# First score tile of a query half made for plain and latent keys together; first half of the latent keys rotated one head ahead

## The reference

```python
q  = rope(heads(x @ w_q))                  # 32 heads
k  = rope(heads(x @ w_k)); v = x @ w_v     # 8 heads, each used by 4 query heads
lk = rope(heads((x @ w_lq) @ w_lk))        # 32 latent key heads, from a rank-128 projection
lv = heads(x @ w_lv)                       # 32 latent value heads
out = causal_attn(q, k, v) @ w_o + causal_attn(q, lk, lv) @ w_lo
x = x + out                                # then a small layer with a routed low-rank term
```

## Time and profile before

| | |
|---|---|
| median of 3 runs | 2036.75 us (2035.94 to 2037.59) |
| profiled execution | 2036.75 us, span 2035.0 us, granted PE clock 0.998 |
| PE busy | 99% of the span |
| DVE, ACT, POOL busy | 72%, 59%, 44% |
| DMA | 15.7% of 16 engines' span |

### The profile page before, as it was taken

How to read it: one execution, slowest core, us unless ns; L and a number is a source line. 1 busy time by engine, 2 the same in 40 slices (tenths; PEclk the granted TensorE clock), 3 DMA queues, 4 the chain that set the end, 5 groups by cost and what they waited for, 6 DMA issues and landing times.

```text
span 2035.0 us, 33416 instructions
## 1 busy us (share of the span) xinstructions
PE 2018.2 (99%) x11716; PEld 1753.1 (86%) x11716; DVE 1457.1 (72%) x2884; ACT 1203.7 (59%) x2505; POOL 889.9 (44%) x684
## 2 busy tenths in 40 slices
PE   8999999999999999999999999999999999999989
PEld 7888888888888888888888888888888888888877
DVE  7677776776777767777677776777776776777777
ACT  4666556565565656666566565666566565565651
POOL 5444544444443454444534454444544444443422
PEclk9999999999999999999999999999999999999999
DMA  3111111111111111112111111111111111111031
GB/s 108 47 34 44 48 28 38 34 49 37 38 39 39 33 44 37 44 28 49 33 44 37 39 39 28 49 34 44 48 28 41 32 49 39 37 39 38 23 68 42
DMA packets 101797, 83.78 MB, mean 41 GB/s; under 512 B 28152, under 2 KB 73848, under 8 KB 101632
## 3 DMA queue, kind: packets, MB, share of 16 engines
q1 hardware_dynamic: 101632, 81.65, 15.7%
HBM read 79.26 MB, written 2.36 MB: 40 GB/s over the span
## 4 chain that ended last, share of the span: by engine, by line
PE 97%; DVE 2%; ACT 1%; POOL 0%; issue 0%; DMA 0%; DVEq 0%; ACTq 0%
PE bankT L587 13%; PE scores L514 12%; PE scores L516 12%; PE scores L515 12%; PE bankX L514 9%; PE bankX L516 9%; PE bankX L515 9%; PE bankO L516 7%; PE bankO L515 7%; PE bankO L514 7%; PE scores L707 0%; PE scores L553 0%; DVE rot_half L1124 0%; DVE xnT_lo L1097 0%; ACT probs L876 0%
## 5 line engine op out<-in xcount | busy, mean ns | idle before, releaser
L815 ACT ACTIVATE PT_hi<-bankT 128x512 fp32r<-128x512 f32 (+2 forms) x640 | 337.5, 533 | 310.7 <-PE bankO L516 275.5
L1113 DVE TENSOR_TENSOR PT_lo<-bankT,PT_hi 128x512 fp32r<-128x512 f32 (+2 forms) x640 | 388.1, 607 | 175.7 <-ACT PT_hi L815 173.1
L876 ACT ACTIVATE probs<-probs,nmax 128x128 f32<-128x128 f32 (+7 forms) x512 | 393.9, 771 | 129.8 <-DVE nmax L1107 129.7
L1107 DVE CUSTOM_DVE_ANT_0 probs<-scores,mask 128x128 f32<-128x128 f32 (+7 forms) x512 | 379.2, 750 | 69.3 <-PE scores L516 68.0
L587 PE MATMUL bankT<-ident,probs 128*128 128x128 f32 x2304 | 382.7, 275 | 6.8 <-ACT probs L876 5.0
L587 PEld LDWEIGHTS bankT<-ident,probs 128*128 128x128 f32 x2304 | 279.6, 140 | 67.9 <-DVE PT_lo L1113 11.7
L1369 POOL TENSOR_TENSOR rot<-rot,cos 128x512 f32<-128x512 f32 x144 | 186.9, 1298 | 256.6 <-DVE rot_half L1124 256.6
L1363 POOL TENSOR_TENSOR OT_lo<-o_raw,OT_hi 128x512 fp32r<-128x512 f32 x63 | 98.3, 1560 | 319.9 <-ACT OT_hi L815 319.9
L815 ACT ACTIVATE OT_hi<-o_raw 128x512 fp32r<-128x512 f32 x128 | 146.7, 1146 | 139.7 <-DVE o_raw L1182 139.7
L1371 POOL TENSOR_TENSOR rot<-rot,rot_half 128x512 f32<-128x512 f32 x144 | 199.9, 1388 | 11.3
L1123 DVE TENSOR_TENSOR rot_half<-rot,sin 64x512 f32<-64x512 f32 x144 | 99.5, 691 | 135.3 <-ACT rot L815 132.3
(11 more groups left out here) (304 smaller groups left out, 5334.0 us busy)
## 6 DMA issues: line engine op xcount, KB each, us to landing
inv_b<-inverses SPq DMA_DIRECT2D x128, 256.0 KB, 3.9
stage<-in_L_attn_w_q SPq DMA_DIRECT2D x32, 256.0 KB, 4.8
stage<-in_L_attn_w_lv SPq DMA_DIRECT2D x32, 256.0 KB, 2.9
stage<-in_L_attn_w_o SPq DMA_DIRECT2D x32, 256.0 KB, 3.5
stage<-in_L_attn_w_lo SPq DMA_DIRECT2D x32, 256.0 KB, 2.6
acc<-in_L_attn_hidden_states SPq DMA_DIRECT2D x8, 256.0 KB, 4.9
stage<-in_L_attn_w_k SPq DMA_DIRECT2D x8, 256.0 KB, 5.0
stage<-in_L_attn_w_v SPq DMA_DIRECT2D x8, 256.0 KB, 5.0
```

What stands on the lines that cost most here:

```text
L815: return act.activation(place, src, ACT.Copy)
L876: act.activation(prob_tile(c, t), prob_tile(c, t), ACT.Exp, bias=nmax[:, c, t:t + 1], scale=-1.0, accum_out=rsum[:, c, t:t + 1]).then_inc( ...
L1107: dve.tensor_tensor_reduce(place, src, tile_view(mask[:, S - width:S], c), -SCALE, -MASKED, ALU.add, ALU.min, nmax[:, c, t:t + 1]).then_in ...
L1113: dve.tensor_tensor(pt_place(1, hh, w, j), bankT[j % 2][:, block_columns(c, j):CH], f32(pt_place(0, hh, w, j)), ALU.subtract).then_inc(pt_ ...
```

## The change

Names in it: `LKA` is half 0 of the *next* head's latent keys, made ahead.

- For all heads but the first, the piece LK half 0 leaves window 0, slot 0; the same projection, as LKA, stands in window 2, slot 0 of the head before. So do its steps: `rope_take` on ACT after the exponentials of slot 0, `rotate` on DVE at the end of slot 2, `rope_add` on POOL ahead of Q half 0's and behind `Wlo_lo`, `rope_high` on ACT in window 3, slot 0, `rope_low` on POOL ahead of Q half 0's.
- The keys lie side by side (`keys_T`), so that one `mm3` of 256 columns makes the first tile for both kinds in window 3, slot 4. The latent tile leaves window 1, slot 1; its `row_max` and `exp_tile` move behind those of the plain tile, into an own buffer `probs_ahead`.
- `Wlk` is loaded third-last to second in a head: order `Wq, Wlk, (Wlv0,) Wo, Wlo, (Wlv1)`. ACT copies it in window 1, slot 2 (slot 5 in the last head of a group), where it stood in window 3, slot 5. `Wlv0` is issued after the second `spread_inverses` in place of before it.
- Tiles are numbered by `TILE_NO` in the order in which they are made.

```diff
     if w == 0:
-        return {0: ("LK", 0), 1: ("LK", 1), **({3: ("LV", 0)} if more else {})}
+        return {**({0: ("LK", 0)} if (g, hh) == FIRST else {}), 1: ("LK", 1), **({3: ("LV", 0)} if more else {})}
...
-        return {**ahead, 3: ("Q", 0)} if more else {}
+        return {**ahead, 0: ("LKA", 0), 3: ("Q", 0)} if more else {}
...
-    return ["Wq", "Wlv0", "Wo", "Wlo", "Wlk", "Wlv1"]
+    return ["Wq", "Wlk", "Wlv0", "Wo", "Wlo", "Wlv1"]
...
+def tiles_at(g, hh, w, s):
+
+    if w == NW - 1 and (g, hh) == FINAL:
+        return []
+    to = (g, hh, w + 1) if w < NW - 1 else (*divmod(g * GROUP + hh + 1, GROUP), 0)
+    tiles = []
+    for t in range(TPC):
+        if TILE_SLOTS[w][t] == s:
+            if t or w != 1 or (g, hh) == FIRST:
+                tiles.append((*to, t))
+            if t == 0 and w == NW - 1:
+                tiles.append((*to[:2], 2, 0))
+    return tiles
...
+                if (w, t) == (0, 0) and (g, hh) != FIRST:
+                    mm3(scores[0][:, 0, 0:2 * P].rearrange("p (k n) -> p k n", k=2), query,
+                        both(keys_T, ALL, ALL, slice(0, P)), True, True).then_inc(scored, 2)
+                    return
...
+            highs = [{(0, 3): ("LK", 0), (1, 0): ("LK", 1), (3, 0): ("LKA", 0), (3, 1): ("Q", 0), (3, 3): ("Q", 1)}
...
                         if here.get(s - 1, ("", 0))[0] == "LK":
                             piece(g, hh, w, s - 1, *here[s - 1], piece_bank(g, hh, w, s - 1))
+                        if here.get(s - 2, ("", 0))[0] == "LKA":
+                            piece(g, hh, w, s - 2, *here[s - 2], piece_bank(g, hh, w, s - 2))
...
                     if w == 2 and more:
+                        rope_add(rope_no(g, hh, "LKA", 0), rope_no(g, hh, "LKA", 0) % RING, 0)
                         rope_add(rope_no(g, hh, "Q", 0), rope_no(g, hh, "Q", 0) % RING, 0)
                     if w == 3 and more:
+                        rope_low(rope_no(g, hh, "LKA", 0), rope_no(g, hh, "LKA", 0) % RING, LKT, (ALL, chunk(0)))
                         rope_low(rope_no(g, hh, "Q", 0), rope_no(g, hh, "Q", 0) % RING, QT, q_at(0))
```

More of the change, by code:

```diff
@@ L81, in loads_of, with number_tiles @@
     if hh % 2:
-        return (["Wk", "Wv"] if hh == GROUP - 1 else []) + ["Wq", "Wo", "Wlo", "Wlk"]
+        return (["Wk", "Wv"] if hh == GROUP - 1 else []) + ["Wq", "Wlk", "Wo", "Wlo"]
     if (g, hh) == (KVH - 1, GROUP - 2):
-        return ["Wq", "Wo", "Wlo", "Wlk"]
-    return ["Wq", "Wlv0", "Wo", "Wlo", "Wlk", "Wlv1"]
-ROPE = ("Q", "K", "LK")
+        return ["Wq", "Wlk", "Wo", "Wlo"]
+    return ["Wq", "Wlk", "Wlv0", "Wo", "Wlo", "Wlv1"]
[11 more added lines that the diff above has]
+    return tiles
+def number_tiles():
+    order = [(*FIRST, 0, t) for t in range(TPC)]
+    for g in range(KVH):
+        for hh in range(GROUP):
+            for w in range(NW):
+                for s in range(BLOCKS[w]):
+                    order += tiles_at(g, hh, w, s)
+    last, ahead = [None, None], {}
+    for at in order:
+        ahead[at] = last[at[3] % 2]
+        last[at[3] % 2] = at
+    return {at: no for no, at in enumerate(order)}, ahead
+TILE_NO, AHEAD_IN_SCORES = number_tiles()
+ROPE = ("Q", "K", "LK", "LKA")
 X_BEFORE = 10
@@ L463, in group_of_heads @@
                         else:
[L464 removed]
+                            fetch("Wq", "Wlk")
                     if not more:
@@ L610, in piece @@
                     mm = mm3(bankX[:, :], both(Wlk, ALL, ALL), both(lqT, ALL, slice(n * CH, n * CH + CH)), True, True)
+                elif name == "LKA":
+                    pe.wait_ge(w_lo, load_no(g, hh, "Wlk") + 1)
+                    mm = mm3(banksX[bank], both(Wlk, ALL, ALL), both(lqT, ALL, slice(0, CH)), True, True)
                 elif name == "LV":
@@ L901, in group_of_heads @@
                                       piece_bank(g, hh, w, s))
-                        early = s + 2 < BLOCKS[w] and name in ("", "LK", "OUT0", "OUT1")
+                        early = s + 2 < BLOCKS[w] and name in ("", "LK", "LKA", "OUT0", "OUT1")
                         if early:
                             block_hi(g, hh, w, s + 2)
[L905 to L909, removed]
+                        for at in tiles_at(g, hh, w, s):
+                            exp_tile(*at)
+                        if name in ("Q", "K", "LKA"):
                             rope_take(n_piece(g, hh, w, s), rope_no(g, hh, name, n), rope_no(g, hh, name, n) % RING,
@@ L958, in group_of_heads @@
                             fetched(g, hh, name, places)
-                        if w == 3 and s == 5 and more:
-                            fetched(g, hh, "Wlk", Wlk)
                         if w == 3 and s == 6 and "Wlv1" in loads_of(g, hh):
@@ L1363, in subtract, with rope_add @@
                 return pool.tensor_tensor(place, src, f32(hi), ALU.subtract)
-            def rope_add(no, slot, n, place=None):
-                half = n if place is None else place
+            def rope_add(no, slot, n):
+                half = no % 2
                 pool.wait_ge(rope_half, no + 1)
```

139 lines of the change are left out of this document (76 added, 63 removed).

## The result

| | before | changed |
|---|---|---|
| median, range of the runs | 2037.17 us, 2035.94 to 2038.56 | 2146.90 us, 2144.81 to 2149.18 |
| ratio | | 1.0539, interval 1.0520 to 1.0557 |
| span of the profiled execution, clock | 2035.0 us, 0.998 | 2145.1 us, 0.995 |

A forecast was written before the change was run, and what follows sets the result against it. PE bounds the kernel, busy 99% of the span. From 2036.75 us: -15.8 tile, +0.9 merged tile, +1.5 first PV, +72.9 stalls (31 x 2.35), -3.0 last head give 2093.2 us; range 2080 to 2108, or 2045 to 2118 without hidden case and clock.

The forecast's parts named there:

- the sum: All terms added to the profiled execution's 2036.75 us, giving 2093.2 us, 2.8% slower.
- What PE saves: Window 1, slot 1: without the latent tile PE saves 0.51 us in each of 31 heads, -15.8 us.
- The first PV of window 0: Moving LK half 0 out uncovers this matmul's wait: 0.05 us a head, +1.5 us, bounds 0 and 0.3.
- Step 1: Q half 0's rotate on DVE meets LKA's cos product on POOL: DVE is 1.05 us late.
- Step 2: DVE ends PT_lo 0 at 334.80, PV at 334.96 just in time; scale_out ends at 335.40.
- Step 3: OT_lo on DVE and POOL's sum for Q half 0 compete; DVE taken first, ending at 337.78, no further loss.
- a rival at 3.0 us a head in slot 3: POOL's sum goes before OT_lo, so window 3's stall is 3.0 us a head: 2113 us; chance 0.12.
- The last head of a group: It has V half 1 in window 2 but the same queue; sketch gave 2.8 us, 2.35 kept.
- Steps 4 and 5: Q half 1's rotate waits for POOL, PT_lo 3 ends at 341.85; window 3 slot 3's transposes wait 2.35 us a head.
- Last head: Window 0 of the kernel's final head: without LK half 0's rotate, -3 us, bounds 0 and -6.
- The clock: Rival: 2.35 us waits lower the clock in half the heads, 2 to 3 us each: 2133 us; chance 0.06.

The follow-up runs named there:

- e1: Changed kernel, but the first latent score tile is made by itself in window 1 again, its keys still rotated a head ahead: 2156.07 us.
- e12: Changed kernel with LKA in window 1, its rotate behind the last row_max, Q half 0 rotated from PSUM, DVE reordered, LK half 1 in window 0 slot 0: 2025.96 us.
- e3: Changed kernel, but POOL's sum of Q half 0 waits for DVE's OT_lo of the same window: 2123.64 us.
- e4: Changed kernel, but at each window's end DVE runs scale_out ahead of PT_lo 0 instead of behind it: 2101.38 us.
- e5: Changed kernel without LKA's two rotating products on DVE and two rope_add instructions on POOL (output differs): 2116.7 us.
- e13: Changed kernel without LKA's rotate on DVE, rope_add on POOL and POOL's subtraction for LKA (output differs): 2042.02 us.
- e8: Changed kernel with scale_out before PT_lo 0, Q half 1's rotate behind PT_lo 3, Q half 0's reading PSUM in heads 0 to 2, window 3's banks swapped there: 2045.60 us.
- e2: Changed kernel, but Q half 1's two rotating products on DVE read the rows from PSUM instead of the SBUF copy: 2115.34 us.

## Why the prediction was wrong

The direction was right, and so was what makes DVE late: its two-input instructions and POOL's wait for each other. Where that reaches PE was not. A plain head has two stalls more than the sum, in slots 0 and 2 of window 3, a third (the first PV of window 0) is ten times its price, and the one that the sum has is smaller. Steps 2 and 3 give the times at which `scale_out` and `OT_lo` end, but they don't ask which matmul waits for them: that is the step that failed.

- **What PE saves.** -0.51 at that place, as forecast, but e1 gives the merge only 0.30 of it. The 0.13 us that the prediction reads for a step of 128 columns has the tile's short wait in it; without the wait it is 0.28 / 3 = 0.09.
- **The first PV of window 0.** Taken as 0.05, bounds 0 and 0.3. It was 0.55. The step named only `PT_lo` as what this PV needs. It writes `bankO`, so it also needs `scale_out` to have read it, and that stands behind `PT_lo` 0 on DVE: 627.19 + 0.68 = 627.87, PV at 628.01. The rows of the kernel before had it: `scale_out` ends there at 349.86 + 0.68 = 350.54, and PV starts at 350.70, 0.16 behind it, where it starts 0.14 behind it in the changed kernel with a wait. So there was nothing to spare already.

```profile
349.86 0.68 DVE L1182 TENSOR_TENSOR o_raw<-bankO,inv_b 128x512 f32<-128x512 f32 x1
```

  That is about 15 us more in 31 heads than the sum has; most of what taking LK half 0 out of window 0 gave is given back. e12, which covers the place again, gains 8.9 us.
- **Step 1** (1.05 late from LKA's cos product): right, 1.69 in place of 0.69.
- **Step 2** ("PV at 334.96: just in time"): failed. The same omission, `scale_out`: the step itself has it end at 335.40, 0.44 behind that PV. The transposes of block 2, which wait for `PT_lo` 0, are late too: 0.62 us a plain head together, some 0.5 a last one, 19 in all.
- **Step 3**, the race. "Ready within 0.01 us", and I took DVE first. POOL went first (`OT_lo` 2.04 us). I had this as a rival at 3.0 us a head in slot 3. But its first effect is elsewhere, and this is the largest miss: **PE's output projection in window 3, slot 2, needs `OT_lo`**, and comes 1.40 us later for it in each plain head, some 33 us in 24 heads (28.7 us of it show as waits). The prediction looked for places where PE is near another engine and named two; this was a third, and nearer than `QT_lo`. In the kernel before, `OT_lo` ends at 334.93 + 1.10 = 336.03, and PE starts 0.15 later, the same 0.15 as in the changed kernel, where it waits (612.06 to 612.21):

```profile
336.18 0.47 PE L514 MATMUL scores<-Wo_hi,OT_lo 128*128 128x512 f32 x1
```

  With the shift of 0.70 that matmul is due at 336.88. Step 3 has `OT_lo` end at 337.78 in its good case and at 338.84 in the other, so a wait here followed from its own numbers, 0.9 or 2.0 us. e3 cuts this wait to 0.3 us, e4 removes it.
- **The last head of a group** was given the same 2.35. Its window 3 has no wait for `OT_lo`, and none for `PT_lo` 3; PE waits 1.80 to 1.83 us for `V_lo`, which stands behind Q half 1's `rotate` on DVE (12.7 us in seven heads).
- **Steps 4 and 5.** The collisions of Q half 1's `rotate` are there (0.95 and 1.68 us), though it is `QT_lo` and not LKA's subtraction that runs ahead of the second product. The stall was 1.27, not 2.35. PE comes to it 2.07 us later than before, where the sum had 0.70 - 0.51 = 0.19: the unpriced waits ahead absorbed 1.88 of it. Against that, `PT_lo` 3 itself ends 3.3 us later than before (counted as in the table; 616.13 against 582.96), where the sum had 3.02 - 0.51 = 2.5. So 2.35 - 1.88 + 0.8 = 1.27. Of the causes named for it, POOL's subtraction in step 4 is enough by itself: with the work of steps 1 to 3 left out the stall is 1.88 us (e5), without the subtraction too it is nothing (e13).
- **Last head.** -3 against -3.3 (the 3.8 less the tile's 0.5). The size is right, but the exponential there still keeps PE waiting for 1.60 us after 2.02. What got shorter is the stretch at the lower clock: 0.80 and 0.52 in 1940 to 1945 and 1945 to 1950 before, 0.98 and 0.68 in 2050 to 2055 and 2055 to 2060 now. No run here tests what shortened it.
- **The clock.** A rival at 0.06 that partly came in. In all seven last heads of a group PE waits 1.8 us for `V_lo`, and in four of them the granted clock then falls from 1.00 to 0.69 in the stretch behind, PE being busy all through it (columns as for e5):

```profile
808.00:811.50 3.50, 1.75 (x10) 1.14 (x8) 3.46 (x4) 1.25 (x3) 2.68 (x3) 1.00 0.09 31
811.50:817.00 5.50, 5.45 (x23) 4.62 (x24) 3.73 (x11) 1.61 (x3) 3.19 (x3) 0.69 0.08 28
```

Those heads take 4.8 to 5.1 us more than before, the other three 3.3 to 3.6: about 6 us. Plain heads with waits of 1.25 and 1.22 us keep 61.45. In one plain head the waits of window 3 come as 1.20, 0.27 and 1.86 us; the granted clock behind them is 0.53 from 419.7 to 423.3, and the head takes 2.5 us longer than the others. Together the clock has some 9 of the 110 us. In e5, where the wait was 1.88 us, 10 of 23 plain heads did the same, at 1.54 us each; in e3 and e4, where the waits for `V_lo` are 1.54 and 1.46 us, no last head did. So the rival named the right thing: stalls of 1.8 to 1.9 us, somewhat shorter than the forecast's, cost clock now and then. Why four of seven equal waits did and three did not, no run shows. The Trainium skill, TensorE: Matmul & The Clock Gate, section The HAM clock gate, has the clock follow how busy PE has lately been, between 1.2 and 2.4 GHz; the trace agrees in so far as PE is busy for 1.75 of the 3.5 us ahead of the slow stretch, whose 0.69 is a mean of the two levels (from 812.0 to 815.4 alone it is 0.55).

The rule of the Trainium skill, SBUF — State Buffer, section Who interferes with whom, held wherever it was tested: 1.68 us against 0.69 with two SBUF inputs, and 0.69 beside POOL once one of them is in PSUM (e8; e2 in the same way).

## What to carry to other kernels

For a PE that is busy 99%, list for every matmul all the semaphores it depends on, the buffer that it overwrites included, and the slack of each, before pushing an engine back by a microsecond: here a delay of 1 to 2 us on DVE met four such places, not two. Every time that a hand calculation gives for the end of an instruction should be laid against the matmul that reads its result. Walk the delay through in order, since a stall at one place pays part of the next. And a queue's order is worth trying before anything is given up: putting `PT_lo` 3 and `scale_out` ahead of work that nobody needs soon gave back 80 of the 110 us, though the same order cost 11 us in the kernel before.

## What the hardware showed that I had not expected

- A turn lost by 0.11 us costs about a microsecond: `OT_lo` takes 2.04 us when POOL's sum starts just ahead of it, 1.10 when free.
- When a two-input instruction of DVE and one of POOL are both waiting, the engines take turns, instruction by instruction: in e5 two subtractions on POOL make both products of one `rotate` last 1.58 and 1.67 us. So it matters less how long POOL's queue is than how many of its instructions stand beside DVE's two-input ones: one subtraction of 1.3 us on POOL is worth 75 us in the whole kernel (e5 against e13), 15 of them by the clock.
- 128 columns beside 256: the tile took 0.28 us when nothing made it late (e1), less than the 0.35 of a 256-column tile, though nowhere near half.
